# Partner rows of queries and keys by DMA and a GpSimd multiply, in place of a permutation matmul and a VectorE product

## The reference, cut to what matters

```python
q, k, v = split(layernorm(x) @ w_qkv.T + b_qkv)      # (b, 16 heads, 512, 8)
q = elu(q) + 1.0;  k = elu(k) + 1.0
q = rope(q); k = rope(k)     # x1 = even channels, x2 = odd channels
                             # even: x1*cos - x2*sin   odd: x1*sin + x2*cos
attn = softmax(q @ k.T * scale) @ v
x = x + layernorm(attn + depthwise_conv(v))
x = x + layernorm(experts(layernorm(x)))
```

## Time and profile before

| | us |
|---|---|
| median of 3 timed runs | 1349.93 (1349.86 to 1350.73) |
| the profiled execution, its own time | 1361.09 |
| span in that profile (first to last instruction) | 1359.3 |
| attention, from its first value product to that of slot 1 of iteration 15 | 100 to 872 |
| busy over the span: PE, DVE, ACT, POOL | 82%, 79%, 69%, 62% |

### The profile page before, as it was taken

The page is one execution under the profiler, slowest core; times in us unless marked ns, Lnnn a source line. Parts: engine busy times, 40 slices in busy tenths (PEclk is TensorE's granted clock), DMA queues, the critical chain, the costliest instruction groups (busy, mean ns, idle before and its releaser), DMA issues. The chain is left out here.

```text
span 1359.3 us, 22331 instructions
## 1 busy us (share of the span) xinstructions
PE 1119.0 (82%) x6568; PEld 478.2 (35%) x6568; DVE 1078.1 (79%) x2483; ACT 944.2 (69%) x1748; POOL 839.2 (62%) x1145
## 2 busy tenths in 40 slices
PE   2599999999999999999999998971799897777710
PEld 0122222232232222332322222221588685556510
DVE  2589999999999999999999999623667575898644
ACT  1028888887887887887888787860699784776511
POOL 5244366566676876877777775545477436885555
PEclk9559999999999999999999999985899997999965
DMA  2462241241242341342332331002234533444312
GB/s 61 89 173 65 60 103 50 65 111 50 73 119 57 96 117 44 93 98 64 89 87 72 87 88 47 19 20 93 84 122 144 172 122 103 128 140 130 86 32 76
DMA packets 104009, 119.89 MB, mean 88 GB/s; under 512 B 13217, under 2 KB 80965, under 8 KB 103621
## 3 DMA queue, kind: packets, MB, share of 16 engines
q1 hardware_dynamic: 93728, 97.55, 26.5%
q0 software_dynamic: 8192, 16.79, 4.5%
q10 hardware_dynamic: 1968, 4.13, 0.8%
HBM read 58.91 MB, written 59.51 MB: 87 GB/s over the span
## 5 line engine op out<-in xcount | busy, mean ns | idle before, releaser
L922 DVE TENSOR_REDUCE MX<-psS 128x1 f32<-128x512 f32 x1024 | 651.2, 679 | 67.1 <-PE psS L423 61.1
L678 ACT ACTIVATE PR<-psST 128x512 f32<-128x512 f32 x986 | 536.7, 599 | 133.6 <-PE psST L411 124.9
L423 PE MATMUL psS<-KS,QS 48*128 48x512 bf16 x1024 | 362.4, 401 | 33.7 <-DMA KS<-scratch_parts 18.5
L411 PE MATMUL psST<-QS,KS 51*128 51x512 bf16 x986 | 335.7, 388 | 24.5 <-ACT PR L678 8.5
L437 PE MATMUL psPV<-PR,V 128*32 128x512 f32 x2048 | 276.8, 613 | 7.4 <-ACT OT L592 2.2
L411 PEld LDWEIGHTS psST<-QS,KS 51*128 51x128 bf16 x986 | 77.5, 93 | 382.2 <-ACT PR L678 337.4
L1707 POOL DMA_INDIRECT GOT<-scratch_y,FROM x128 | 129.3, 1010 | 38.3 <-issue 35.9
L423 PEld LDWEIGHTS psS<-KS,QS 48*128 48x128 bf16 x1024 | 84.9, 93 | 88.9 <-DVE MX L922 62.7
L1033 POOL DMA_INDIRECT scratch_x<-XN,POSI x96 | 95.4, 994 | 26.7 <-issue 26.6
L1382 PE MATMUL psH<-XH,WS 128*128 128x512 f32 x184 | 83.2, 452 | 16.9 <-ACT XH L1434 6.8
L1384 PE MATMUL psH<-XH,WS 128*128 128x512 f32 x184 | 75.7, 411 | 0.0
(11 more groups left out here) (173 smaller groups left out, 2004.8 us busy)
## 6 DMA issues: line engine op xcount, KB each, us to landing
scratch_parts<-PT SPq DMA_DIRECT2D x192, 128.0 KB
QS<-scratch_parts SPq DMA_DIRECT2D x64, 192.0 KB, 3.5
KS<-scratch_parts SPq DMA_DIRECT2D x64, 192.0 KB, 4.4
XR<-scratch_x SPq DMA_DIRECT2D x46, 256.0 KB
scratch_y<-YR SPq DMA_DIRECT2D x46, 256.0 KB
scratch_x<-ZERO SPq DMA_DIRECT2D x18, 256.0 KB
X<-in_x SPq DMA_DIRECT2D x16, 256.0 KB, 5.0
scratch_turned<-XT SPq DMA_DIRECT2D x16, 256.0 KB, 4.5
```

The source lines that it names most:

```text
L411: nc.tensor.matmul(bank(st_banks(t), k)[:], KS[t.par][rows, h // 2, kc * P:(kc + 1) * P], QS[t.par][rows, h // 2, :], start=True, stop=Tru ...
L423: nc.tensor.matmul(bank(psS, k)[:], QS[b.par][rows, h // 2, qc * P:(qc + 1) * P], KS[b.par][rows, h // 2, :], start=True, stop=True).then_ ...
L678: nc.scalar.activation(PR[:, s % 2, j, :], bank(st_banks(t), k)[:], ACT.Exp, scale=SCALE).then_inc(st_exp, 1)
L922: nc.vector.tensor_reduce(out=MX[:, qc, h:h + 1], in_=bank(psS, k)[:], axis=AX.X, op=ALU.max).then_inc(s_max, 1)
```

## The change

The product with `PERM` and the product on VectorE are gone, and so are `PERM` itself and its load. In their place SP issues, for queries and for keys each, two DMAs from SBUF to SBUF with 64 partitions of 2 KB: even rows of `RES` get the odd rows of `EL`, odd rows the even ones. It waits for `EL[w]`, and stands in SP's order after the load of x and ahead of the maxima. GpSimd multiplies `RES` in place by `SIN`, ahead of each of its two sums. The minus sign of the even channels has moved into the table `SIN`.

```diff
 # SyncE, iteration(t)
                 if (t + 3).live:
                     load_x(t + 3)
+                b, b2 = t + 1, t + 2
+                if b2.live:
+                    turn(b2, 0)
+                    turn(b2, 1)
                 if t.live:
                     store_max(t, 1)
...
+            def turn(b, w):
+                sp.wait_ge(qk_elu[w], b.done(1, 1))
+                if due(before := b.done(1, 0)):
+                    sp.wait_ge(part3[w], before)
+                for odd in range(2):
+                    sp.dma_start(RES[odd::2, w, :], EL[1 - odd::2, w, :]).then_inc(turned[w], 16)
 # TensorE, misc(t, s)
-                if s in (5, 6) and prep.live:
-                    w = s - 5
-                    use = ("Rq", "Rk")[w]
-                    misc_freed(pe, t, use)
-                    pe.wait_ge(qk_elu[w], prep.done(1, 1))
-                    nc.tensor.matmul(misc_bank(use)[:], PERM[:], EL[:, w, :], start=True, stop=True)...
 # VectorE, elu(b, w): may EL be written again?
-                    dve.wait_ge(rot_psum[w], before)
+                    dve.wait_ge(turned[w], 32 * before)
 # VectorE, extra(t, s, j)
-                if s in (6, 7) and j == 0 and prep.live:
-                    w = s - 6
-                    dve.wait_ge(rot_psum[w], prep.done(1, 1))
-                    if due(before := prep.done(1, 0)):
-                        dve.wait_ge(part3[w], before)
-                    nc.vector.tensor_tensor(RES[:, w, :], misc_bank(("Rq", "Rk")[w])[:], SIN[:], ALU.mult)...
 # GpSimd, iteration(t)
                     for w in range(2):
+                        pool.wait_ge(turned[w], prep.done(32, 32))
+                        nc.gpsimd.tensor_tensor(RES[:, w, :], RES[:, w, :], SIN[:], ALU.mult).then_inc(rot_sin[w], 1)
                         pool.wait_ge(rot_cos[w], prep.done(1, 1))
                         pool.wait_ge(rot_sin[w], prep.done(1, 1))
                         nc.gpsimd.tensor_tensor(ROT[:, w, :], ROT[:, w, :], RES[:, w, :], ALU.add)...
 # constants
-        NCONST = 14
+        NCONST = 13
-        MISC = ["xT", "q", "k", "mT1", "O3", "Rq", "Rk", "O0", ...
+        MISC = ["xT", "q", "k", "mT1", "O3", "O0", ...
+    sin = sin * np.where(np.arange(C) % 2 == 0, -1.0, 1.0).astype(np.float32)[:, None]
```

More of the change, by code:

```diff
@@ L96, in constant, with attention @@
         first += size
-def attention(nc, x_in, wqkvT, chan, ones, rope_cos, rope_sin, perm, ident, numbers, count, gate_wT, gate_b,
+def attention(nc, x_in, wqkvT, chan, ones, rope_cos, rope_sin, ident, numbers, count, gate_wT, gate_b,
               X, IDF, TAB, ZERO, BD, XN2, POS, POSI, WSEL, CW, BASE, CNT, XG, XTD, scattered, zero_filled, table, load_weights):
@@ L112, in attention @@
         WQKV = sb("WQKV", [P, 3 * C], F32)
-        PERM = sb("PERM", [P, P], F32)
         IDB = sb("IDB", [P, P], BF16)
@@ L197, in attention @@
         qk_elu = [sem(f"qk_elu{w}") for w in range(2)]
-        rot_psum = [sem(f"rot_psum{w}") for w in range(2)]
+        turned = [sem(f"turned{w}") for w in range(2)]
         rot_cos = [sem(f"rot_cos{w}") for w in range(2)]
@@ L237, in attention @@
         GATE_STEPS = 26
-        NCONST = 14
+        NCONST = 13
         LOADS = 2 * 16 * 2
-        MISC = ["xT", "q", "k", "mT1", "O3", "Rq", "Rk", "O0", "lepeT", "mT0", "O1", "vT", "xT2", "V",
+        MISC = ["xT", "q", "k", "mT1", "O3", "O0", "lepeT", "mT0", "O1", "vT", "xT2", "V",
                 "O2", "lg"]
@@ L249, in attention @@
         READER = {"xT": (2, xT_ready, 1, 1), "mT1": (0, mT_ready, 2, 2), "q": (2, qk_elu[0], 1, 1),
-                  "O3": (-1, o_norm, 4, 4), "k": (2, qk_elu[1], 1, 1), "Rq": (2, rot_sin[0], 1, 1),
-                  "Rk": (2, rot_sin[1], 1, 1), "O0": (0, o_norm, 4, 1), "lepeT": (-1, y_ready, 1, 1),
+                  "O3": (-1, o_norm, 4, 4), "k": (2, qk_elu[1], 1, 1),
+                  "O0": (0, o_norm, 4, 1), "lepeT": (-1, y_ready, 1, 1),
                   "mT0": (1, mT_ready, 2, 1), "O1": (0, o_norm, 4, 2), "V": (1, v_ready, 1, 1),
@@ L316, in iteration @@
                     load_x(t + 3)
-                b = t + 1
+                b, b2 = t + 1, t + 2
+                if b2.live:
+                    turn(b2, 0)
+                    turn(b2, 1)
                 if t.live:
@@ L321, in iteration @@
                     stack_max(t, 1)
-                b2 = t + 2
                 if b2.live:
@@ L468, in misc @@
                     out_transposes(prev, 3, "O3")
-                if s in (5, 6) and prep.live:
-                    w = s - 5
-                    use = ("Rq", "Rk")[w]
-                    misc_freed(pe, t, use)
-                    pe.wait_ge(qk_elu[w], prep.done(1, 1))
-                    nc.tensor.matmul(misc_bank(use)[:], PERM[:], EL[:, w, :], start=True, stop=True).then_inc(rot_psum[w], 1)
                 if s == 7 and t.live:
@@ L571, in _ @@
         def _(act):
-            for dst, src in ((IDF[:], ident), (WQKV[:], wqkvT), (CHAN[:], chan), (PERM[:], perm),
+            for dst, src in ((IDF[:], ident), (WQKV[:], wqkvT), (CHAN[:], chan),
                              (COS[:], rope_cos), (SIN[:], rope_sin), (GW[:], gate_wT),
@@ L730, in extra @@
                     normalise(prev, 3, "O3")
-                if s in (6, 7) and j == 0 and prep.live:
-                    w = s - 6
-                    dve.wait_ge(rot_psum[w], prep.done(1, 1))
-                    if due(before := prep.done(1, 0)):
-                        dve.wait_ge(part3[w], before)
-                    nc.vector.tensor_tensor(RES[:, w, :], misc_bank(("Rq", "Rk")[w])[:], SIN[:],
-                                            ALU.mult).then_inc(rot_sin[w], 1)
                 if s == 8 and j == 1 and t.live:
@@ L1735, in _, with build @@
                     rsqrt(FINISH.index(p - 2))
-def build(nc, x, wqkvT, chan, ones, cos, sin, perm, ident, table, count, gate_wT, gate_b, w1T, w3T, wdT, b2, out):
+def build(nc, x, wqkvT, chan, ones, cos, sin, ident, table, count, gate_wT, gate_b, w1T, w3T, wdT, b2, out):
     ctx = ExitStack()
@@ L1786, in unit_table @@
                         table_step, expert_ready, row_ready)
-        attention(nc, x, wqkvT, chan, ones, cos, sin, perm, ident, table, count, gate_wT, gate_b,
+        attention(nc, x, wqkvT, chan, ones, cos, sin, ident, table, count, gate_wT, gate_b,
                   X, IDF, TAB, ZERO, BD, XN2, POS, POSI, WSEL, CW, BASE, CNT, XG, XTD, scattered, zero_filled, unit_table, load_weights)
@@ L1811, in host_constants @@
     count = np.where(np.stack([before, np.ones((P, P), bool)], 1), 0x3F80, 0).astype(np.uint16)
-    return dict(cos=cos, sin=sin, perm=perm, ident=np.eye(P, dtype=np.float32), table=table, count=count)
-_INPUTS = ("x", "wqkvT", "chan", "ones", "cos", "sin", "perm", "ident", "table", "count", "gate_wT", "gate_b",
+    return dict(cos=cos, sin=sin, ident=np.eye(P, dtype=np.float32), table=table, count=count)
+_INPUTS = ("x", "wqkvT", "chan", "ones", "cos", "sin", "ident", "table", "count", "gate_wT", "gate_b",
            "w1T", "w3T", "wdT", "b2")
```

## The result

| | before | after |
|---|---|---|
| median of 5 timed runs, us | 1350.73 (1349.86 to 1352.15) | 1337.51 (1334.52 to 1341.93) |
| ratio | | 0.9904, 95% interval 0.9886 to 0.9923 |
| the profiled execution, us | 1361.09 | 1338.71 |
| its span, us | 1359.3 | 1336.9 |
| first value product of iteration 0, at | 99.96 | 97.83 |

The change saves 13.2 us (10.4 to 15.4 by the interval), where 8.7 were forecast; 1337.5 lies in the range. The sign held, and so did the mechanism in the main: what was off are the sizes of two terms, and behind one of them a hold that the forecast hadn't looked for.

The account below looks back on a forecast made before the run. It took a per-slot floor to bound ungated iterations and VectorE's stream gated ones; 4.5 + 3.5 - 1.0 - 1.5 + 2.7 + 0.45 = 8.65 us off 1349.93 gave 1341.2 us, range 1333 to 1348.5.

Parts of the forecast that it names:

- Ungated iterations: Nine iterations (0 to 3, 5, 7, 9, 11, 13): slots 5 to 7 fall to the floor, 0.5 us each, 4.5 us.
- The floor read from iteration 14: Slots 5 to 7 without rotation products take 8.65 us, 2.88 a slot, so three slots can give back 0.49 us.
- VectorE is the bound everywhere: Rival: all fourteen iterations gain VectorE's full 1.2 us, with the start 18.45 us, giving 1331.5 us; chance 0.17.
- Gated iterations: Iterations 4, 6, 8, 10, 12: VectorE saves 1.2 us each, less 0.5 for GpSimd holding gate operations; 3.5 us in all.
- GpSimd and slot 7's copy: ScalarE's copy of ROT ending slot 7 waits some 0.5 us in iterations 6, 8, 10, 12; half charged, 1.0 us lost.
- that rival: GpSimd late for slot 7's copy in iterations 5 to 13: each us later costs up to nine, 1355.7 us; chance 0.10.
- The copies: The DMAs from SBUF to SBUF take 2 to 3 us and cost nothing in steady state, covered by slots 4 and 5.
- The start: Before iteration 0: 1.5 us lost in iteration -2, 2.7 gained in iteration -1, 0.45 from the constant; 1.65 us gained.
- The constant's load: One DMA issue less in the row whose last landing starts the kernel's work: 0.45 us gained.
- Iteration -1: At the 1.2 GHz clock, without permutation products VectorE sets the pace: 7.8 us become 5.1, 2.7 us gained.
- The gain is eaten in place: Rival: ungated iterations give 0.25 us, gated ones nothing, the start 0.5; 1347.7 us, about no change; chance 0.18.
- VectorE's idle time before its maxima: Sign in the profile after: this idle time grows from 16.6 us by several us, VectorE's saving being mostly off the path.

Follow-up runs that it names:

- c_before: The kernel before, unchanged, run again on another chip for a second trace: median 1329.48 us, ratio to before 0.9999.
- c_after2: The kernel after, unchanged, run again on the same chip as c_before: median 1317.81 us, ratio to before 0.9914.
- e_pe: The kernel after with a dummy matmul put back in slots 5 and 6, its product unused: 1322.52 us, ratio to before 0.9944.
- e_dve: The kernel after with a dummy VectorE product put back in slots 6 and 7, its result unused: 1329.28 us, ratio to before 0.9999.
- h_late_scatter: The kernel after with GpSimd's first four scatter DMAs moved behind the two sums of the rotation: 1321.30 us, ratio to before 0.9946.
- e_both: The kernel after with both dummies put back, the matmul and the VectorE product, results unused: 1332.01 us, ratio to before 1.0014.
- c_after: The kernel after, unchanged, run again on a third chip where runs scatter more: 1344.89 us, ratio to before 0.9931.
- e_nodma: The kernel after without the DMA copies of rows, GpSimd multiplying EL itself by SIN: 1341.31 us, ratio to before 0.9899.
- e_twomul: The kernel after with one more GpSimd multiply of the same shape ahead of each multiply by SIN: 1358.99 us, ratio to before 1.0027.

## Why the prediction was right, and where its sizes were off

The terms, forecast against the quiet pair (c_before less c_after2, iteration by iteration):

| term | forecast | measured |
|---|---|---|
| start: iteration -2, iteration -1, constant | -1.5 + 2.7 + 0.45 = 1.65 | -1.7 + 3.4 + 0 = 1.7 |
| ungated iterations 0 to 3 | 4 x 0.5 = 2.0 | 1.8 |
| ungated iterations 5, 7, 9, 11, 13 | 5 x 0.5 = 2.5 | 3.7 |
| gated iterations, less slot 7's copy | 3.5 - 1.0 = 2.5 | 5.8 |
| iteration 14 | 0 | 0 |
| from slot 1 of iteration 15 to the end | 0 | -0.8 |
| sum | 8.65 | 12.2 |

**Ungated iterations: right.** The floor read from iteration 14 was reached to 0.01 us, and e_pe and e_dve show what stood above it: two loads side by side, each worth the same 0.5 us. The rival *VectorE is the bound everywhere* (1.2 us in each iteration) is refuted. The extra 0.4 us in iterations 7 and 9 isn't in slots 5 and 6. It is in slots 2 to 4: 10.10 us in iteration 7 of c_before, 9.68 in c_after2. It is a hold too, on one more gate operation with two inputs in SBUF, which falls in slot 1 of the iterations behind the gated ones. c_before, VectorE and GpSimd:

```profile
457.77 0.96 DVE L897 TENSOR_TENSOR PICK<-OH,RANK 128x128 f32<-128x128 bf16 x1
457.32 1.26 POOL L999 TENSOR_TENSOR LP<-LP,TAP 128x512 f32<-128x512 f32 x1
```

c_after2:

```profile
452.16 0.51 DVE L892 TENSOR_TENSOR PICK<-OH,RANK 128x128 f32<-128x128 bf16 x1
451.25 1.27 POOL L994 TENSOR_TENSOR LP<-LP,TAP 128x512 f32<-128x512 f32 x1
```

In both it ends 0.15 us after GpSimd's sum of the convolution, and in c_before that sum stands later against VectorE's stream. The operation takes 0.96, 0.91, 0.70 and 0.91 us in iterations 7, 9, 11 and 13 of c_before and 0.50 to 0.51 in c_after2. Slots 2 to 4 follow it: 10.10, 10.04 and 9.83 us in iterations 7, 9 and 11 against 9.68, and 10.27 in h_late_scatter, where it takes 1.14. In e_both, which has the old load back but no GpSimd waiting for VectorE's products (12.2 us of waiting in 400 in c_before), it takes 0.52 and the slots 9.68. So this part of the saving, about 1.1 us in four iterations, comes from GpSimd being on time and not from the two removed products. In the first trace of before, where slot 14 of the iteration ahead is late, the operation takes 0.52 too. I had not reckoned with a saving that is paid out one iteration later.

**Gated iterations: the term that was mis-sized most.** I charged 0.5 us each for GpSimd's hold on the gate operations and 0.25 in four of them for the copy. VectorE in iteration 8 of c_before (timeline; the four gate operations of the first round):

```profile
525.52 0.85 DVE L837 TENSOR_TENSOR CAND<-BI,TOP 128x64 f32<-128x64 f32 x1
...
526.89 0.68 DVE L737 TENSOR_TENSOR RES<-psM,SIN 128x512 f32<-128x512 f32 x1
...
528.69 0.38 DVE L840 TENSOR_TENSOR CAND<-CAND,TAB 128x64 f32<-128x64 f32 x1
...
531.99 0.80 DVE L846 TENSOR_TENSOR OH<-TAB,TOP 128x64 bf16<-128x64 f32 x1
...
533.32 0.65 DVE L849 SCALAR_TENSOR_TENSOR BI<-OH,BI 128x64 f32<-128x64 bf16 x1
```

and of c_after2:

```profile
518.39 0.21 DVE L832 TENSOR_TENSOR CAND<-BI,TOP 128x64 f32<-128x64 f32 x1
...
520.32 0.91 DVE L835 TENSOR_TENSOR CAND<-CAND,TAB 128x64 f32<-128x64 f32 x1
...
524.16 0.24 DVE L841 TENSOR_TENSOR OH<-TAB,TOP 128x64 bf16<-128x64 f32 x1
524.92 0.22 DVE L844 SCALAR_TENSOR_TENSOR BI<-OH,BI 128x64 f32<-128x64 bf16 x1
```

Holds moved about. I had looked only at the two operations that I expected to meet the new multiplies, and had not counted the holds that the kernel before already had later, at `OH` and `BI`. With both rounds, these four groups take 3.40 us in iteration 8 of c_before and 3.36 in c_after2: the net hold is nil. So VectorE's 1.20 us should come through whole, and iterations 8 and 12 gained 1.15. Only in iteration 4, which has no scatters and so another alignment, do the same groups go from 2.74 to 3.37 us: there the charge was real, 0.63. (The Trainium skill, "SBUF — State Buffer", Who interferes with whom, says that a VectorE instruction with two SBUF inputs contends with a GpSimd instruction that reads SBUF. The rows agree: in iteration 8 of c_after2 `CAND<-BI,TOP` takes 0.21 us in one round and 0.78 in the other. It is the count of meetings that I had wrong.)

The rest is TensorE's clock. Windows around slots 9 and 10, c_before in iteration 10:

```profile
635.00:640.00 5.00, 3.85 (x24) 1.01 (x22) 5.00 (x11) 4.53 (x10) 3.31 (x4) 1.00 0.31 84
640.00:645.00 5.00, 5.00 (x29) 1.33 (x29) 4.99 (x15) 3.17 (x7) 1.39 (x2) 0.66 0.20 54
```

c_after2 in iteration 4:

```profile
320.00:325.00 5.00, 3.77 (x25) 0.89 (x24) 5.00 (x11) 4.10 (x9) 3.27 (x4) 1.00 0.40 110
325.00:330.00 5.00, 5.00 (x29) 1.36 (x29) 4.79 (x14) 2.98 (x7) 1.29 (x2) 0.66 0.19 52
```

Here, after a slot in which TensorE waits for VectorE (busy 3.8 of 5 us), the granted clock, at 2.4 GHz before, has a mean of 0.66 over the next 5 us, so part of them was at 1.2 GHz. Iteration 8 of c_before has the same slot 9, 4.29 us, and no fall. Slot 10 takes 4.19 us where it takes 3.43 without the fall: 0.75 us. Between slots 1 of iterations 1 and 15, c_before has two falls (iterations 6 and 10) and before two (6 and 12); after, c_after and c_after2 have one each, in iteration 4. The account closes: 5 x 1.20 - 0.63 + 0.75 x (2 - 1) = 6.1 us against 5.8 measured. Of what the forecast of 2.5 missed, the hold is 1.9 us (2.5 charged, 0.6 found), the copy 1.0 (see below) and the one fall less 0.75. The falls go with the kernel in these five traces, but e_pe and e_nodma have none in that stretch, and what decides it was not shown.

**GpSimd and slot 7's copy: right, and the price too high.** The wait came where it was put, 0.51 us in iteration 8 against 0.5 reckoned, 1.7 us in 400 in all. It cost nothing: iterations 8 and 12 gained all but 0.05 us of VectorE's share. It decides from just beyond, as e_twomul shows: 1.25 us more makes 14 us, about what the "nine us" for each us of that rival gives (9 x 1.25 = 11.3, and 3.0 at the start).

**The copies: right.** 2.0 us from issue to landing at the median against 2 to 3 reckoned, no wait by GpSimd between 300 and 700 us, and nothing gained without them that could be told from scatter.

**The start: right in sum.** The first scores of iteration -1 come 1.71 us later (45.53 and 47.24; forecast 1.05 with the constant), iteration 0 begins 1.70 earlier (forecast 1.65). The constant's load brought nothing in the quiet pair: VectorE's first statistics start at 10.69 and 10.70. Iteration -1 gave 3.4 us in place of 2.7. VectorE in c_before:

```profile
64.71 1.26 DVE L922 TENSOR_REDUCE MX<-psS 128x1 f32<-128x512 f32 x2
67.15 0.69 DVE L922 TENSOR_REDUCE MX<-psS 128x1 f32<-128x512 f32 x1 [1.19 <-PE psS L423]
67.76 0.68 DVE L737 TENSOR_TENSOR RES<-psM,SIN 128x512 f32<-128x512 f32 x1
```

and in c_after2:

```profile
66.43 12.09 DVE L917 TENSOR_REDUCE MX<-psS 128x1 f32<-128x512 f32 x20
```

Two products of 0.6 and the pauses of 1.19 and 0.85 us before the maxima after each matmul make 3.2; I had reckoned from one row to another across them and come out half a us short.

**The rival** *The gain is eaten in place* (1347.7) fails with the net hold of nil. One mark that I named was wrong: VectorE's idle time before its maxima was to grow from 16.6 us and fell to 14.7; from c_before to c_after2 it grew, 12.1 to 15.1. Between two executions this row moves more than by the change.

**Open.** In the first trace of before, slots 6 and 14 of iterations 5 to 12 were longer than in c_before by up to 0.9 us, and slot 12 of iteration 13 by 1.1. The same lengthening shows in all four traces of the chip of c_after, and in none of the seven of the chip of c_before; after has it in iteration 13 alone. So it doesn't go with the kernel. It makes most of the 5.7 us by which the first pair's saving up to iteration 15 (18.7) exceeds the quiet pair's (13.0). What makes it wasn't found. Nor did I find out when the clock falls in a gated iteration and when it doesn't.

## What to carry to other kernels

Read a floor from an iteration that lacks the work in question: a slot's saving is bounded by it, and not by the busy time removed. Where one engine's stream sets the end, price its removed instructions in full, and count interference from another engine over the whole round of operations, before and after, and in the iteration behind it, not only where the new work falls. GpSimd, off the critical path here, took work up to an edge and then charged for it in nine iterations; one dummy instruction more on such an engine finds that edge.

## What was not expected of the hardware

- The clock record of after reads 1.00 all through the first 100 us, where before read 0.50 from 40 to 100. The matmuls say otherwise: the projection of queries in iteration -1 of after takes 2.07 us for its two passes (below; the next matmul starts 2.00 us behind it), as long as before's permutation products at a record of 0.50, against 2 x 0.644 in the middle of attention. In such a stretch durations are to be trusted, not the record.

```profile
52.54 2.07 PE L550 MATMUL psM<-XT,WQKV 128*128 128x512 f32 x2
```

- The kernel before took 1350.7, 1329.6 and 1356.3 us in the median on three chips. From slot 1 of iteration 15 to the end, before took 487.5 us and c_before 463.0; attention up to there differed by 7.1 only. The difference between those two executions is thus mostly behind it. The ratio moved far less: 0.9904, 0.9914, 0.9931.
- A copy from SBUF to SBUF of 64 partitions with 2 KB each is issued in 0.7 us (2.81 for four) and lands 2.0 us after its issue at the median.
